# The last gather of a graph network: deeper message buffers, earlier indices, and GpSimd tied to TensorE at every fourth group

## The reference, cut to what matters

```python
def spline_conv(x, row, col, basis, idx, W, b):
    z = einsum('ni,kio->nko', x, W).reshape(N * K, Fout)     # K = 125, Fin = Fout = 32
    gathered = z[col[:, None] * K + idx]                     # 8 corners of a cell for each edge
    msg = einsum('es,eso->eo', basis, gathered)              # weighed by 8 basis values
    out = segment_sum(msg, row, num_segments=N)              # summed by the edge's source node
    deg = segment_sum(ones_like(msg[:, 0]), row, num_segments=N)
    return out / maximum(deg, 1.0)[:, None] + b
```

## Time and profile before

| | us |
|---|---|
| median of 3 runs | 11856.13 |
| lowest and highest of them | 11834.23, 11860.02 |
| the profiled execution, its own time | 11889.0 |
| its span, first to last instruction | 11887.2 |

### The profile page before, as it was taken

The page is one execution under the profiler, slowest core; times in us unless marked ns, Lnnn a source line. Parts: engine busy times, 40 slices in busy tenths (PEclk is TensorE's granted clock), DMA queues, the critical chain, the costliest instruction groups (busy, mean ns, idle before and its releaser), DMA issues. The chain is left out here.

```text
span 11887.2 us, 143975 instructions
## 1 busy us (share of the span) xinstructions
PE 5759.6 (48%) x32326; PEld 4601.4 (39%) x32455; DVE 6368.5 (54%) x16774; ACT 3373.4 (28%) x7561; POOL 6278.5 (53%) x8257
## 2 busy tenths in 40 slices
PE   4232233434556666466666466666433333742222
PEld 2111133333434344355555466666233333422222
DVE  6444555554411111466656788888455555645555
ACT  0000022222133333111111577777311112321111
POOL 3777566664155555455555344444155555046665
PEclk8555555655566666566666555555655555865555
DMA  6331222211555555222223799999211111776666
GB/s 192 111 111 57 60 56 58 57 55 51 189 184 192 178 192 188 43 68 67 68 64 65 278 349 350 349 350 346 76 38 37 37 38 36 285 260 206 196 204 182
DMA packets 895764, 1760.16 MB, mean 148 GB/s; under 512 B 488178, under 2 KB 488487, under 8 KB 891096
## 3 DMA queue, kind: packets, MB, share of 16 engines
q0 software_dynamic: 317952, 1023.05, 26.8%
q1 hardware_dynamic: 538584, 598.40, 15.0%
q10 hardware_dynamic: 39168, 138.04, 2.9%
HBM read 1150.49 MB, written 611.50 MB: 148 GB/s over the span
## 5 line engine op out<-in xcount | busy, mean ns | idle before, releaser
L1771 POOL DMA_INDIRECT got<-corners,now x1664 | 1606.8, 966 | 1812.6 <-DVE now L1757 768.7
L1771 POOL DMA_INDIRECT got<-node_rows,now x1664 | 1607.3, 966 | 1689.4 <-issue 1327.2
L1771 POOL DMA_INDIRECT got<-patches,now x832 | 794.1, 954 | 906.2 <-issue 625.0
L948 POOL DMA_INDIRECT d_rows<-row x832 | 834.8, 1003 | 545.8 <-issue 534.6
L1677 PE MATMUL made_p<-weights,turned 64*128 64x320 f32 x2450 | 792.7, 639 | 564.9 <-ACT z L1701 297.9
L2574 PE MATMUL sum_p<-msg_s,hot_s 128*128 128x64 f32 x3328 | 737.2, 423 | 597.0 <-DVE msg_s L2029 597.0
L699 POOL DMA_INDIRECT s_rows<-row_now,pos_i x784 | 758.0, 967 | 373.7 <-issue 363.5
L2574 PEld LDWEIGHTS sum_p<-msg_s,hot_s 128*128 128x128 f32 x3328 | 717.6, 332 | 605.9 <-DVE msg_s L2029 605.9
L2113 PE MATMUL acc_p<-msg,hot_s 128*128 128x32 f32 x1664 | 376.2, 402 | 984.8 <-DVE msg L2037 808.0
L1819 DVE TENSOR_TENSOR a<-a,sum_p 128x64 f32 x832 | 183.6, 221 | 1246.4 <-remote 727.1
L1701 ACT COPY z<-made_p 128x384 f32<-128x384 f32 x1225 | 525.4, 489 | 976.5 <-DMA d_rows<-row 471.2
(11 more groups left out here) (423 smaller groups left out, 15024.2 us busy)
## 6 DMA issues: line engine op xcount, KB each, us to landing
corners<-z SPq DMA_DIRECT2D x245, 960.0 KB
corners<-z SPq DMA_DIRECT2D x98, 864.0 KB
d_rows<-empty ACTq DMA_DIRECT2D x32, 1586.0 KB
row<-d_rows SPq DMA_DIRECT2D x104, 488.0 KB
corners<-z SPq DMA_DIRECT2D x49, 672.0 KB
s_rows<-empty ACTq DMA_DIRECT2D x32, 962.0 KB
row<-s_rows SPq DMA_DIRECT2D x104, 296.0 KB
got<-node_rows,now POOLq DMA_INDIRECT x1664
```

What stands on the lines that cost most here:

```text
L948: pool.indirect_dma_start(out=d_rows, out_offset=bass.IndirectOffsetOnAxis(ap=to[:, t, DPOS:DPOS + 1], axis=0), in_=row[b][:, t, :], in_of ...
L1771: pool.indirect_dma_start(out=to[b][:, t, :], out_offset=None, in_=table, in_offset=bass.IndirectOffsetOnAxis(ap=indices.now[b][:, t:t + 1 ...
```

## The change

The messages and both forms of the one-hots get four buffers instead of two, `prod` one instead of two, and `rows` is laid into `prod`. `Corners.sum` is split into `weigh` and `add`. VectorE's order for group `g` becomes: wait for landing and weights, weigh, copy the indices of group `g+4`, wait for group `g-4` of TensorE, one-hot, add. `summed` starts at 6, so that it stands at 7 more than the last group done. GpSimd waits, at the first of every four groups, `4i`, for `summed` at `4i+2`, which is group `4i-5` of TensorE (for the first round: the clearing of the sums).

```diff
 class PsumColumns:
-    def __init__(self, k, ph):
+    def __init__(self, k, ph, rows=None):
         self.k = k
-        self.rows = sb(k, ph, "rows", [LO, T, LO], BF16)
+        self.rows = sb(k, ph, "rows", [LO, T, LO], BF16) if rows is None else rows
...
-    def sum(self, dve, c, at, weights, prod, msg):
+    def weigh(self, dve, c, at, weights, prod):
         for n in range(4):
             m = dve.tensor_tensor(prod[:, :, 2 * n:2 * n + 2, :], self.corner(at, n // 2, n % 2, 0, 2),
                                   last(weights[:, :, 2 * n:2 * n + 2], self.C), ALU.mult)
         c.after(m)
+
+    def add(self, dve, prod, msg):
         return dve.tensor_reduce(msg[:], prod[:].rearrange("p t c f -> p t f c"), AX.X, ALU.add)
...
-        msg = [sb(k, ph, "msg", [LO, T, C]) for _ in range(2)]
-        hot_s = [sb(k, ph, "hot_s", [LO, T, LO]) for _ in range(2)]
-        hot16 = [sb(k, ph, "hot16", [LO, LO, T], BF16) for _ in range(2)]
+        msg = [sb(k, ph, "msg", [LO, T, C]) for _ in range(4)]
+        hot_s = [sb(k, ph, "hot_s", [LO, T, LO]) for _ in range(4)]
+        hot16 = [sb(k, ph, "hot16", [LO, LO, T], BF16) for _ in range(4)]
...
-        prod = [sb(k, ph, "prod", [LO, T, 8, C]) for _ in range(2)]
+        prod = sb(k, ph, "prod", [LO, T, 8, C])
...
-        column = PsumColumns(k, ph)
+        column = PsumColumns(k, ph, prod[:].bitcast(BF16)[:, :, 0:2, :].rearrange("p t c f -> p t (c f)"))
...
                         pool.wait_ge(indices.ready, i * 4 + (b + 1))
                         pool.sem_inc(seen, 1)
+                        if b == 0:
+                            pool.wait_ge(summed, i * 4 + 2)
+                            pool.sem_inc(seen, 1)
                         gather(pool, got, conv.table, indices, i, b, gathered, spare=spare)
...
-                indices.first(dve)
+                for g in range(4):
+                    indices.put(dve, g, g)
                 column.begin(dve)
...
                     for b in range(4):
                         g, b2 = i * 4 + b, b % 2
-                        indices.put(dve, g + 3, (b + 3) % 4)
-
-                        dve.wait_ge(summed, g)
-                        one_hot(dve, hot16[b2][:], column.of[:], k.lo_s[:, tiles(g)]).then_inc(hot, 1)
                         gathered.wait(dve, b, i + 1)
                         dve.wait_ge(weighed, g + 1)
-                        corners.sum(dve, c, got[b], weight[b2], prod[b2], msg[b2]).then_inc(based, 1)
-                dve.wait_ge(summed, G + 2)
+                        dve.wait_ge(based, g + 2)
+                        corners.weigh(dve, c, got[b], weight[b2], prod)
+                        indices.put(dve, g + 4, b)
+
+                        dve.wait_ge(summed, g + 3)
+                        one_hot(dve, hot16[b][:], column.of[:], k.lo_s[:, tiles(g)]).then_inc(hot, 1)
+                        corners.add(dve, prod, msg[b]).then_inc(based, 1)
+                dve.wait_ge(summed, G + 7)
...
-                clear_sums(k, acc_p, 4).then_inc(summed, 1)
+                clear_sums(k, acc_p, 4).then_inc(summed, 6)
...
-                            m = nc.tensor.matmul(at_block(acc, now[t]), hot_s[b2][:, t, :], msg[b2][:, t, :],
+                            m = nc.tensor.matmul(at_block(acc, now[t]), hot_s[b][:, t, :], msg[b][:, t, :],
                                                  start=False, stop=False)
...
-        k.spline_i = sb(k, None, "spline_i", [LO, (G + AHEAD) * T], I32)
+        k.spline_i = sb(k, None, "spline_i", [LO, (G + AHEAD + 1) * T], I32)
```

More of the change, by code:

```diff
@@ L2045, in spline_phase @@
         got = [sb(k, ph, "got", [LO, T, conv.SPAN * C]) for _ in range(4)]
-        msg = [sb(k, ph, "msg", [LO, T, C]) for _ in range(2)]
-        hot_s = [sb(k, ph, "hot_s", [LO, T, LO]) for _ in range(2)]
-        hot16 = [sb(k, ph, "hot16", [LO, LO, T], BF16) for _ in range(2)]
+        msg = [sb(k, ph, "msg", [LO, T, C]) for _ in range(4)]
+        hot_s = [sb(k, ph, "hot_s", [LO, T, LO]) for _ in range(4)]
+        hot16 = [sb(k, ph, "hot16", [LO, LO, T], BF16) for _ in range(4)]
         acc_p = pb(k, ph, "acc_p", [LO, 4, 512])
         acc = acc_p[:].rearrange("p a (h f) -> p (a h) f", f=C)
-        prod = [sb(k, ph, "prod", [LO, T, 8, C]) for _ in range(2)]
+        prod = sb(k, ph, "prod", [LO, T, 8, C])
         weight_p = [pb(k, ph, f"weight_p{b}", [LO, 512]) for b in range(2)]
         weight = [w[:, 0:T * 8].rearrange("p (t x) -> p t x", x=8) for w in weight_p]
-        column = PsumColumns(k, ph)
+        column = PsumColumns(k, ph, prod[:].bitcast(BF16)[:, :, 0:2, :].rearrange("p t c f -> p t (c f)"))
         hot, based, weighed, widened, summed, own, seen = ph.sems("hot", "based", "weighed", "widened", "summed", "own", "seen")
         gathered = Landings(ph, "gathered", 4)
-        indices = Indices(k, ph, k.spline_i)
+        indices = Indices(k, ph, k.spline_i, 4)
         corners = Corners(C)
@@ L2098, in _ @@
                         act.wait_ge(hot, g + 1)
-                        nc.scalar.copy(hot_s[b % 2][:], hot16[b % 2][:].rearrange("p l t -> p t l")).then_inc(widened, 1)
+                        nc.scalar.copy(hot_s[b][:], hot16[b][:].rearrange("p l t -> p t l")).then_inc(widened, 1)
             @block.tensor
@@ L2103, in _ @@
                 column.turn(pe)
-                clear_sums(k, acc_p, 4).then_inc(summed, 1)
+                clear_sums(k, acc_p, 4).then_inc(summed, 6)
                 with pe.Fori(0, QUADS) as i:
                     for b in range(4):
-                        g, b2 = i * 4 + b, b % 2
+                        g = i * 4 + b
                         load_blocks(k, pe, k.of_src, g)
```

## The result

The changed kernel took 11713.81 us (median of four runs, 11710.72 to 11753.43) and the kernel before 11858.08 (four runs, 11834.23 to 11863.4): the ratio is **0.989, [0.9876, 0.9904]**, 144 us less where 160 were forecast (11696), and inside the range of 11615 to 11785. The profiled execution of after is its slowest, 11753.43 us with a span of 11751.6; beside the profiled execution of before (11889.0) it is 136 us shorter.

The account below looks back on a forecast made before the run. GpSimd's gather issue rate was taken as the floor, 1100 us, with stalls above it. Terms -245 + 71 + 4 + 10 = -160 us, from the median 11856, gave 11696 us; range 11615 to 11785.

Parts of the forecast that it names:

- The stalls and their cause: Last gather: some 245 us of GpSimd stalls, because TensorE's "done" reaches VectorE late while GpSimd streams gathers.
- B: VectorE's one_hot is shut out by a port lock until GpSimd stops; no change, 11856 us within 24; chance 7%.
- C: At GpSimd's new wait the work is undone: 12.1 us at each of 25 boundaries, 11928 us; chance 5%.
- A: No pauses in the last gather, every increment needed passes in time: 241 us off, 11615 us; chance 10%.
- Step 1: VectorE's one_hot waits four groups back: increments may be 34 us late unnoticed, against some 11 before; not everything covered.
- Step 2: VectorE copies indices for group g+4 before the one_hot's wait, which takes 6.8 us out of the stall.
- Steps 3 and 4: GpSimd's wait at every fourth group: 17 pauses of 4.2 us, 71 us in all.
- step 4: How many of GpSimd's 25 boundaries pause: two in three, as increments still pass for a while after a resume.
- rival D: Longer gather streams choke: half of 104 groups cost 1.7 us more, 88 us of gain go, 11784 us; chance 6%.
- Start and end: First gather waits for the clearing of the sums, 4 us lost; VectorE works off held groups after the last, 10 us.

Follow-up runs that it names:

- e7: Kernel before with only the four buffers and single prod, old order, no GpSimd wait: 11762.97 us, ratio 0.9908 to the kernel before on the same chip.
- e5: The whole change, unaltered, run again beside the kernel before: 11735.02 us, ratio 0.9891.
- p4: Kernel before with only GpSimd's wait at every fourth group added: 9882.09 us, ratio 1.0003 to the kernel before on the same chip.
- p1: Changed kernel without GpSimd's wait at every fourth group: 9878.6 us, ratio 1.0003 to the kernel before on the same chip.
- e10: Changed kernel without GpSimd's memsets of the spare tile, where increments are late: 11552.38 us, ratio 0.9925 to the kernel before on the same chip.

## Why the prediction was right, and where it wasn't

**The stalls and their cause: right.** The increments of TensorE were late, not its matmuls, and VectorE was not shut out. B would have kept the stall at 10 us with any number of buffers; buffers alone took 110 of 245 us away. C would have made the pauses of the change 12 us; they are 4, and only at group 20 was the work undone. A needed no pauses; there are 15.

**Step 1, four buffers: right in kind.** They were said not to cover everything, and didn't (35.0 us of waiting in one go in e7). The prediction gave them no number of their own. One number in this step is off by its own working: the lateness that the kernel before bears is two groups less the 8 us, 21.2 - 8 = 13 us, and not some 11; the sum doesn't use it.

**Step 2, indices behind the weighing: wrong as an explanation.** "This takes the 6.8 us out of the stall" holds for no run: without the wait, the stalls with the new order still go to 11.6 us and aren't fewer (31 late gathers, 150 us, against 22 and 121 in the old order); with the wait, the old order gives the same stretch and the same pauses (16 of them, 63 us, with idle times such as the 4.4 us above). The 6.8 us go when GpSimd stops for TensorE, in either order; for the new order itself no run shows a gain.

**Steps 3 and 4, the pauses: right.** 17 of 4.2 us, 71 in all, were forecast for groups divisible by four; 15 of 4.0, 60 in all, came. For much of the phase they have the rhythm of two boundaries in three that step 4 argued for, and for its reason: group 55's matmuls end at 11168.7, 9.4 us after the resume, their increment is recorded 2 us later, and the boundary of group 60 costs nothing. How many pause varies from execution to execution (13 in e5), so some luck is in how near 15 came to 17. The idle times before the first gather of such a group are 2.55 to 6.06 us, mostly 3.3 to 4.7.

**What was not foreseen: 30 us at other groups.** After six groups without a pause GpSimd stands for about 3 us at the start of the seventh (groups 30, 38, 50, 62, 74, 98), and TensorE gets slow in the streams' last groups. This is rival D in kind, long streams choke, at about a third of its price. The row with 1.65 us was its sign; D was set at 88 us of loss with the forecast at zero for it, and 30 + 10 of smaller gaps would have been the right term. Timeline of after around the pause of group 30, TensorE and GpSimd, and GpSimd's semaphore and register instructions in the gap (duration in ns):

```profile
10849.65 0.21 PE L2121 MATMUL acc_p<-msg,hot_s 128*128 128x32 f32 x1 [2.59 <-issue]
10852.46 0.21 PE L2121 MATMUL acc_p<-msg,hot_s 128*128 128x32 f32 x1 [2.60 <-issue]
```

```profile
10852.89 0.95 POOL L1771 DMA_INDIRECT got<-corners,now  x1 [0.30 <-issue]
...
10857.38 0.95 POOL L1771 DMA_INDIRECT got<-corners,now  x1 [3.26 <-DMA weights<-wide_w]
```

```profile
L121 POOLq EVENT_SEMAPHORE  x1: 699/699/699, 10854.5 to 10854.5; - x1
...
L149 POOLq EVENT_SEMAPHORE  x1: 687/687/687, 10855.9 to 10855.9; - x1
...
L150 POOLq FUSED_REGOPS  x1: 699/699/699, 10856.6 to 10856.6; - x1
```

GpSimd's pause is largely its own small instructions: three that elsewhere take 17 to 37 ns (the medians in this phase) take 2.1 of the 3.26 us. At TensorE a matmul of 0.21 us comes every 2.8 us, and nothing that the profile shows holds it. The name behind the gap of 10857.38 is that of another phase's tensor, so it says nothing of the cause; the indices of group 30 had been copied behind the weighing of group 26.

**Start and end.** The start cost 4.5 us against 4 forecast. The end cost 0.5 against 10: by the last groups VectorE was not behind, the one_hot of the last group following its weighing at once (the matmuls of the last group, 11728.58, come right behind its reduction).

**The sum.** Stalls 245 to 100 instead of to 71: 29 us worse, made of some 40 for the gaps at other places, less 11 for fewer and slightly cheaper pauses. The end: 9.5 us better, the start 0.5 worse. -160 + 29 - 9.5 + 0.5 = -140, and the two profiled executions differ by -136 with 4.9 us from the phases ahead. The largest error in size is the missing term for streams of six groups; the two that cancel hide a part of it.

What none of this foretold is that all of it depends on the chip. A forecast for "the kernel" was a forecast for chips that are late.

**Open.** Why some chips are late and others not; wait alone and order alone where increments are late; whether short gathers would let them pass; whether it is the stream of gathers that holds them; why TensorE's and GpSimd's streams slow. The whole change was not run on a chip that is late with nothing; its parts and the version without memsets cost nothing there. That version (without the spare memsets) is the best run here on the fast kind of chip, 0.995 [0.9936, 0.9963] of the kernel before, and there the only one that beats it. On the other kind it stands at 0.9925 [0.9904, 0.9946] against the change's 0.989 [0.9876, 0.9904] and 0.9891 [0.9872, 0.991], on different chips; its stretch is 9 us shorter, and I don't call it better or worse there. The kernel before itself was not profiled on the fast kind; the nearest to it, p4, has a stretch of 1101.4 us.

## What to carry to other kernels

Where one engine waits for another's "done" although the work behind it ended long ago, look at what GpSimd is doing: on some of the chips here a semaphore of TensorE was tens of us late under a nearly unbroken stream of gathers, and then depth (waiting for work of four groups ago, not of two) is the cheap cure, 110 us of 245 here. If the stream must pause anyway, stop it at a place of your own choice, where the waiting engine still has its inputs: a pause cost 4 us here and an unplanned one 10. Measure such a thing on more than one chip before you explain it or tune to it, and give a forecast the chip that it is for.

## What the hardware showed that was not expected

**One kernel, two kinds of chip.** 11637 to 11880 us on some, 9877 to 9878 on others, the same program. The granted clock is near the same, 0.579 to 0.585 on the former and 0.599 to 0.603 on the latter over the whole program, and 0.50 of full, the lower of its two levels, in this phase on both, in before and p1. Phases differ by 404 us (1539 against 1135) or by nothing (1695 against 1694), the latter where GpSimd's gathers come furthest apart. On p1's chip TensorE's increments come at once, 0.014 to 0.05 us behind, in every phase with gathers.

**Sequencers slow down.** In streams that last, some small instructions of two engines' sequencers (the part that hands an engine its instructions) stretch. In the changed kernel one of TensorE's, issued for every second matmul (duration in ns: min, median, max), and below it the same in p1 on the other kind of chip:

```profile
L2121 PEldq FUSED_REGOPS  x832: 46/46/727, 10533.8 to 11729.4; - x167
```

```profile
L2118 PEldq FUSED_REGOPS  x832: 46/46/51, 8757.3 to 9854.2; - x167
```

GpSimd's increments of a semaphore at L151 go from 17 ns to 727 ns at most in the same phase. They are the more frequent case: 40 of some 207 take over 300 ns, of TensorE's 5 of some 816. In the stretch at one matmul every 2.8 us above, TensorE's recorded small instructions take their usual 46 ns, so these records don't account for its pace. Without the memsets (e10) it is the other way: GpSimd's stay at 17 ns, and 43 of TensorE's go over 300 ns, up to 1384. VectorE's and ScalarE's sequencers kept their pace (at most 75 and 65 ns in after). Before the change this never showed at TensorE (46 to 51 ns in this phase), whose streams were broken by stalls after four or five groups. The Trainium skill (SBUF — State Buffer, Who interferes with whom) says that DMA never contends with a compute engine and that TensorE never waits on anyone. That is said of the memory's ports, and these rows don't show what slows TensorE; but slowed it is, while GpSimd's transfers run.

**Where the increment arrives.** In 22 of the 23 long stalls of the kernel before, the held increments come 0.6 to 1.2 us (0.9 as a median) after GpSimd's queue has sent its last packet, mostly with 0.16 us from one to the next where there are two; one had been held so long that its one_hot came 45 us late.
